# Two expert layers on TensorE: alternating steps against one layer after the other

## The reference, cut to what matters

```python
capacity = max(1, int(N / E * K * CAP_FACTOR))          # 80
buf = zeros((E + 1, capacity, d)).at[e_s, p_s].set(xf[tok])[:E]
h = silu(einsum('ecd,edh->ech', buf, wg)) * einsum('ecd,edh->ech', buf, wu)   # 256 -> 512, twice
out_e = einsum('ech,ehd->ecd', h, wd)                                          # 512 -> 256
gathered = out_e[flat_e, minimum(pos, capacity - 1)]
contrib = gathered * (flat_g * keep)[:, None]
routed = zeros_like(xf).at[tok].add(contrib)
return shared + routed
```

## Time and profile before

| | |
|---|---|
| median of 3 runs | 1791.8 us (1791.11 to 1794.52) |
| the profiled execution, its own time | 1795.56 us |
| its span in the trace | 1793.7 us |
| granted TensorE clock, mean over the span | 0.955 of full speed |
| TensorE matmul busy | 1661.3 us (93%) |
| TensorE weight load busy | 1004.3 us (56%) |
| VectorE busy | 1134.5 us (63%) |
| ScalarE busy | 863.2 us (48%) |
| `up` steps of the stage (line 2128), busy | 155.2 us |
| `down` steps of the stage (line 2144), busy | 98.3 us |

### The profile page before, as it was taken

The page is one execution under the profiler, slowest core; times in us unless marked ns, Lnnn a source line. Parts: engine busy times, 40 slices in busy tenths (PEclk is TensorE's granted clock), DMA queues, the critical chain, the costliest instruction groups (busy, mean ns, idle before and its releaser), DMA issues. The chain is left out here.

```text
span 1793.7 us, 36695 instructions
## 1 busy us (share of the span) xinstructions
PE 1661.3 (93%) x12551; PEld 1004.3 (56%) x12559; DVE 1134.5 (63%) x1997; ACT 863.2 (48%) x1776; POOL 241.4 (13%) x323
## 2 busy tenths in 40 slices
PE   7999969999999998977899999689999999989698
PEld 3444424454454544643777999535454454546597
DVE  6677758888888874626553111188888888836311
ACT  2222215777777774721441111147777777746132
POOL 1321120000000001000101454230000000000000
PEclk9999988999999999998898999889999999999699
DMA  6577765444343417000026999753434344130053
GB/s 193 179 203 209 201 154 92 65 61 69 54 70 59 64 19 174 11 1 1 1 78 227 335 311 318 230 80 63 69 56 70 58 64 64 24 93 5 9 182 103
DMA packets 145444, 193.58 MB, mean 108 GB/s; under 512 B 27401, under 2 KB 119068, under 8 KB 139136
## 3 DMA queue, kind: packets, MB, share of 16 engines
q1 hardware_dynamic: 138680, 188.30, 43.5%
q0 software_dynamic: 4608, 2.18, 0.7%
q10 hardware_dynamic: 2064, 1.87, 0.3%
HBM read 155.42 MB, written 39.97 MB: 109 GB/s over the span
## 5 line engine op out<-in xcount | busy, mean ns | idle before, releaser
L1193 ACT ACTIVATE probs<-ps 128x512 f32<-128x512 f32 x1024 | 558.6, 599 | 199.2 <-PE ps L1103 187.0
L1212 DVE TENSOR_REDUCE top<-ps 128x1 f32<-128x1024 f32 x512 | 603.3, 1219 | 74.6 <-PE ps L1082 61.4
L1103 PE MATMUL ps<-qst,kst 105*128 105x256 bf16 x2048 | 354.0, 276 | 7.6 <-DVE qst L1224 2.3
L1082 PE MATMUL ps<-kst,qst 105*128 105x512 bf16 x1024 | 315.2, 391 | 21.5 <-POOL qst L1007 13.8
L1103 PEld LDWEIGHTS ps<-qst,kst 105*128 105x128 bf16 x2048 | 170.2, 100 | 228.0 <-ACT probs L1193 86.0
L1117 PE MATMUL ps_o<-probs,vst 128*32 128x256 f32 x4096 | 274.1, 385 | 2.3 <-ACT probs L1193 2.3
L1117 PEld LDWEIGHTS ps_o<-probs,vst 128*32 128x32 f32 x4096 | 106.8, 109 | 113.3 <-issue 51.4
L2128 PE MATMUL ps_h<-xe,vall 128*128 128x80 f32 x1024 | 155.2, 273 | 0.0
L2128 PEld LDWEIGHTS ps_h<-xe,vall 128*128 128x128 f32 x1024 | 142.0, 199 | 0.0
L1082 PEld LDWEIGHTS ps<-kst,qst 105*128 105x128 bf16 x1024 | 90.0, 99 | 87.1 <-issue 44.4
L1013 POOL COPY vst<-vall 128x512 f32 (+1 forms) x64 | 39.3, 616 | 708.2 <-PE ps_o L1117 708.1
(11 more groups left out here) (382 smaller groups left out, 1916.1 us busy)
## 6 DMA issues: line engine op xcount, KB each, us to landing
kst<-kd SPq DMA_DIRECT2D x384, 128.0 KB
kd<-kp SPq DMA_DIRECT2D x64, 384.0 KB, 2.8
vall<-in_L_ffn_wg_dram SPq DMA_DIRECT2D x32, 512.0 KB, 6.1
vall<-in_L_ffn_wu_dram SPq DMA_DIRECT2D x32, 512.0 KB, 7.9
vall<-in_L_ffn_wd_dram SPq DMA_DIRECT2D x32, 512.0 KB, 5.6
w<-in_L_ffn_w_dram SPq DMA_DIRECT2D x16, 1024.0 KB, 5.6
ctx_sb<-in_ctx_dram SPq DMA_DIRECT2D x16, 512.0 KB, 5.9
vd<-square_weights SPq DMA_DIRECT2D x16, 512.0 KB, 4.2
```

Source lines behind the costliest of these rows:

```text
L1082: mm = pe.matmul(ps1[:, slot1(m, u), x * 512:(x + 1) * 512], qst[:, m, qt * P:(qt + 1) * P], kst[:, m, c * W1 + x * 512:c * W1 + (x + 1) * ...
L1103: mm = pe.matmul(ps2[:, SCORES2[u], x, :], kst[:, m, kt * P:(kt + 1) * P], qst[:, m, :], start=True, stop=True)
L1193: nc.scalar.activation(probs[:, u % SLOTS, :, :], ps2[:, SCORES2[u], :, :], ACT.Exp).then_inc(probs_ready, 1)
L1212: v.tensor_reduce(top[:, b, u // NC1, u % NC1:u % NC1 + 1], ps1[:, slot1(m, u), :], AX, ALU.max).then_inc(mx, 1)
```

## The change

The rule of the alternation goes. Iteration e now issues all 16 steps of `up(e + 1)` and after them all 8 steps of `down(e)`. The steps, their operands, their signals and their waits are the same, and the loops of the other engines are not touched. One line goes ahead of the loop, so that every line behind it has a number smaller by one.

```diff
@@ -1900,7 +1900,6 @@
     UP, DOWN = 2 * FT0 * C, FT0 * C
-    FIRST_DOWN = 6
@@ -2155,11 +2154,11 @@
                     if e % GE == 1 and e // GE + 2 < NGROUP:
                         table(e // GE + 2)
-                    for s in range(UP):
-                        if e + 1 < E0:
+                    if e + 1 < E0:
+                        for s in range(UP):
                             up(e + 1, s)
-                        if 0 <= s - FIRST_DOWN < DOWN:
-                            down(e, s - FIRST_DOWN)
+                    for s in range(DOWN):
+                        down(e, s)
```

## The result

The changed kernel takes 1804.7 us (median of 4 runs, 1804.16 to 1806.67) against 1793.2 us of before on the same chip (4 runs as well, 1791.11 to 1794.93): ratio 1.0067, with a 95% interval from 1.0049 to 1.0084, that is 9 to 15 us slower. The prediction said 1800.3 us with a range up to 1804.0. The direction and the mechanism of the later iterations were right; the sum was too small, for a reason in iteration 0 that the prediction did not have, and the time lies just outside the range.

The account below looks back on a forecast made before the run. The prediction took TensorE's stream of steps to bound the stage, with DMAs waiting for it. 9.5 us for 30 iterations less 0.95 at the end gave +8.5 us, 1800.3 us from a median of 1791.8, range 1796 to 1804.

Parts of the forecast that it names:

- The bound: In the changed stage TensorE's stream of steps sets the length; PE and PEld have no gap, and DMAs wait for TensorE.
- the rival in which the DMAs hide the loss: Weight loads, with DMA engines 94% busy, set the stage's pace; no change, 1791 to 1793 us; chance 3%.
- the one in which something goes late in every iteration: A fetch or scatter stands late for `turn` in each iteration, 6 us on top, 1806 us; chance 5%.
- The broken pairs: Eight switches from `up` to `down` become one; seven lost at 0.039 us each, 0.27 us an iteration.
- the switch to `turn`: A `down` instead of an `up` row ahead of `turn` loses a cheap switch, 0.045 us an iteration (0 to 0.05).
- The order doesn't matter: Rival: runs cost the same 0.404 us a pair as alternation; only the end wait goes, 1790.6 us; chance 6%.
- step 3: Over 30 iterations with a `turn`, 0.315 us each: 9.5 us slower (6.9 to 10.9), half clock in the first left to the range.
- its rival of a moving clock: A stage ending at another moment shifts the clock's return there and later, a microsecond or two either way; 5%.
- step 4: At the stage's end, `down` steps of expert 30 fill the 1.20 us wait for expert 31's hidden values: -0.95 us.
- nothing is late behind it: After the 1.20 us wait at the last expert goes, no later work is delayed, so the -0.95 us holds.
- 0 to 0.9 us: At the end, expert 31's scatter may wait for expert 29's to land and give this back; taken as 0.
- The sum: Whole kernel: 9.5 - 0.95 = +8.5 us (ends 5.9 and 10.1), 1800.3 us from the median of 1791.8.

Follow-up runs that it names:

- the blocks of two: Kernel before with two `up` steps, then two `down` steps, four times an iteration: 5.31 us from `turn` to `turn`, 1799.3 us in a single run.
- the late pairs: Kernel before with `FIRST_DOWN = 8`, so a `down` step stands ahead of each `turn`: 5.20 us from `turn` to `turn`, 1796.8 us in a single run.
- the narrow steps: Kernel before and changed kernel, each with `down` steps of 64 of the 128 weight columns: 1920.5 and 1859.4 us, a single run each.
- e12_down_first: Changed kernel, but the eight `down` steps of expert 0 go ahead of the 16 `up` steps of expert 1: 1802.32 us.
- the warm kernels: Kernel before and changed kernel, each with 14 matmuls in TensorE's gap ahead of the first `turn`: 1787.53 us (0.9965) and 1794.30 us (1.0007).
- e2_first_runs: Kernel before with only the first iteration (e = 0) in runs of 16 `up` and 8 `down` steps: 1792.76 us, ratio 1.000.

## Why the prediction was wrong, point by point

- *The bound.* Right: PE and PEld stayed without a gap in later iterations, the loads waited for TensorE (110.6 us in 27 waits, 100.9 before), and the rival in which the DMAs hide the loss falls. So does the one in which something goes late in every iteration: after the first tokens no step of TensorE waited for anything.
- *The broken pairs and the switch to `turn` (steps 1 and 2).* Right. 0.315 us an iteration was forecast, 0.30 measured, 8.7 us over 29 iterations (a missing switch 0.037 us and not 0.039, the `turn` 0.04 and not 0.045); the blocks of two and the late pairs gave the lengths expected of each term. The mechanism, the longer of a matmul and the next load, is shown by the narrow steps.
- *The order doesn't matter.* Falls with 5.46 against 5.16 us.
- *Iteration 0.* This is the step that failed, as step 3 put it: "there a broken pair costs double, some 0.15 us more, which I leave to the range". It costs 2.2 us against 0.3 in the sum, since the clock itself comes back later. The prediction took the moment of 979 us as given, and its rival of a moving clock looked only behind the stage. The trace of before had the rows: full clock 3 us after the first `down` step, after 10 us of `up` steps at half. That full clock follows the first `down` steps wherever they stand, and not the first `up` step, is shown by `e12_down_first` and the traces of the others, and the warm kernels show that without the half clock iteration 0 costs 0.31 us. That it shows in the total is not shown, since `e2_first_runs` measured nothing.
- *The last expert (step 4).* -0.95 us forecast, -0.97 measured. But "nothing is late behind it" was wrong: the scatter of expert 31 then waited for that of expert 29, in this trace and in four of the five others that keep the full width and end in runs. Of the "0 to 0.9 us" that might come back, and of which the prediction took 0, it was 0.5 here.
- *The sum.* The time lies 4.4 us above the forecast and 0.7 us above its range. Of the 4.4 us, 1.4 are the base: before had a median of 1791.8 us when the prediction was written and 1793.2 with one run more. Iteration 0 is 1.9 us, the scatter 0.5, the later iterations 0.4 the other way, and about 1 us is in no term. Iteration 0 is the largest of these; without it, or without the shift of the base, the time would have fallen inside the range. With both terms the trace gives 10.4 us, 1802 to 1804 us from medians of 1792 to 1794. Measured were 1804.7 and 1805.3. What is left, up to 3 us, is within the intervals; its cause isn't settled. The part behind the stage differed by up to 6 us between the traces, and the prediction's 1.5 us either way was too little for it, beside a sum that was too low.

## What to carry to other kernels

Where one kind of matmul has the longer load and another the longer stream, alternate them: here each place at which a short stream met a short load saved 0.037 us, and the trace of before tells how much, in a run of each kind and in a stretch of pairs. Where a reordering touches a stretch at half clock, ask what brought the clock back and where that now stands, rather than price its steps at the clock of before. And ahead of the saving of a wait at the end of a chain, ask what the chain waits for next: here, in most traces, a DMA of two experts before.

## What was not expected of the hardware

With `down` steps of 64 columns instead of 128, TensorE had no gap and the clock still stayed at half for over 200 us of the stage (0.50 from 985 to 1230 us in alternation), at a cost of some 127 us against the full-width kernel, for less work. In runs it came back at about 1132 us, without a full-width step; why then is not known. In the nine traces of other kernels with a cold start, full clock came within 4.2 us of the first full-width `down` step, and 14 filler matmuls in a gap of 3 us were worth 6 us.
